# A recommendation tower on one core: tail order, scratch rectangles and batch sizes changed

## The chip, the cores and the metric

The kernel runs on one core of a Trainium2 chip. The metric is the device time of one execution in microseconds; for each kernel several executions are timed and the median is taken. Beside it stands one profiled execution, whose trace gives the start, the length and the waits of each instruction.

## The reference

The inputs are 2048 samples: a dense vector of 128 numbers each, and 26 ids, each naming a row of 128 numbers in its own table (tables of 1000 to 125000 rows). For each sample there are so 27 vectors of 128. What is computed:

```
combined = concat([dense, e_0 .. e_25])            # 27 vectors of 128 per sample
inter    = combined @ combined^T                   # 27 x 27 per sample
z        = concat([dense, inter[upper triangle]])  # 128 + 351
h        = concat([z, dense])                      # 607
h        = relu(h @ W_top1 + b_top1)               # 512
h        = relu(h @ W_top2 + b_top2)               # 256
y        = h @ W_top3                              # 1
```

All of it is in fp32.

## The kernel before, in words

The 2048 samples go through in 8 chunks of 256 (CHUNK), each of two tiles of 128. Of the 27 vectors of a sample, 17 are gathered by GpSimd, one indirect DMA per field and tile (`gather`, line 393), in batches (BATCH_SIZES, line 39); 9 come from small tables kept on chip, looked up by a product of the table with a mask of equal ids (`look_up`, line 429, the masks made by VectorE in `make_masks`); one is the dense vector.

A gathered batch has samples on partitions. TensorE transposes it into one PSUM bank (`turn`, line 415: one transpose for each row of the batch, after `rows_loaded` of the batch and after ScalarE has evicted the batch before), and ScalarE evicts it into `vectors` (`keep_batch`, line 775). So a tile takes five turns and five evictions. GpSimd refills the place of a batch once the batch two tiles back has been turned.

The products of a chunk are made in four steps of 64 samples (`multiply`, line 448: one small product of 27 by 27 for each sample, four samples side by side on the partitions, the "quads"). Step 0 waits for all batches of the chunk's first tile, step 2 for all of the second. Each step is copied into `products` (`keep_step`), by ScalarE but for the very last step, which VectorE copies.

The upper triangle must come to lie with pairs on partitions. For this SP writes `products` to a scratch in DRAM, two rectangles for each quad (`write_quad`, line 215: 26 by 26 and 13 by 13 pairs, each element a run of samples), and loads the 351 pairs back in the order of the first layer's weights (`load_pairs`). For a middle chunk that happens one chunk later than the products: the write starts once the fourth step is kept, and the first layer of chunk i - 1 stands in the middle of chunk i.

The order of each engine's work is written out by hand, as one list for each engine, with waits on semaphores. On TensorE a chunk is: turns of the even tile between look-ups (`chunk`), then `end_of_chunk`: first-layer blocks of the chunk before (`first_layer`, line 465, four of them), step products and turns of the odd tile in alternation, then the second layer, and the last two steps.

The last chunk has a tail of its own (`end`, line 548): its 256 samples go in two halves of 128. The first half is written and loaded as soon as two of four steps are kept (`write_last(0)` and `load_last(0)` on SP); the second half is written by SP (two quads) and ScalarE (two quads) and loaded by SP. `first_of_half` is the first layer of a half in four blocks, `rest_of_half` the second layer and the final product. VectorE keeps the blocks of the first half (`end`, line 690), ScalarE those of the second (`keep_last`, line 838). The output of each half is stored by SP.

Of the kernel before, what the change touches and what calls it, by code (L numbers as in the profile page):

```python
# [16 lines left out]
VECTORS = FIELDS + 1  # L17
DENSE = VECTORS - 1
PAIRS = VECTORS * (VECTORS - 1) // 2
DELTAS = VECTORS // 2  # L20
# [5 lines left out]
LAST = CHUNKS - 1  # L26
# [9 lines left out]
CHUNK_STEPS = TILES * TILE_STEPS  # L36

BATCH_SIZES = (4, 4, 3, 3, 3)
TILE_ROWS = len(GATHERED)  # L40
TILE_BATCHES = len(BATCH_SIZES)
assert sum(BATCH_SIZES) == TILE_ROWS
# [28 lines left out]
MTILES1, MTILES2 = HIDDEN1 // 128, HIDDEN2 // 128  # L71
# [3 lines left out]
HALF = CHUNK // HALVES  # L75
# [4 lines left out]
WRAP = VECTORS + DELTAS - 1  # L80
SLOT = QUADS * CHUNK_GROUPS
SLOTS = VECTORS * WRAP + (VECTORS + 1) * (VECTORS - 1) + 1
FIRST_SLOT = VECTORS * (WRAP - DELTAS)
QUAD_DMAS = 2
SCRATCH_DMAS = QUAD_DMAS * QUADS

# [18 lines left out]
def build(nc, dense, ids, ids_of_field, tables, w1, b1, w2, b2, w3, out):  # L106
    fp32, fp32r, int32 = mybir.dt.float32, mybir.dt.float32r, mybir.dt.int32
    ALU, ACT = mybir.AluOpType, mybir.ActivationFunctionType
# [4 lines left out]
    with ExitStack() as ctx:  # L113
# [101 lines left out]
        def write_quad(engine, c, q, written, half=None):  # L215

            groups = slice(0, CHUNK_GROUPS) if half is None else groups_of(half)

            at = q * CHUNK_GROUPS if half is None else half * HALF + q * HALF_GROUPS
            for rows_, columns, slot in (  # L220
                ((0, VECTORS - 1), (0, VECTORS - 1), VECTORS * (WRAP - VECTORS + 1)),
                ((DELTAS + 1, VECTORS), (VECTORS - DELTAS, VECTORS), (VECTORS + 1) * (DELTAS + 1)),
            ):
                height, width = rows_[1] - rows_[0], columns[1] - columns[0]
                into = bass.AP(scratch[c % 2].tensor, slot * SLOT + at,
                               [[(VECTORS + 1) * SLOT, height], [VECTORS * SLOT, width],
                                [1, groups.stop - groups.start]])
                engine.dma_start(into, products[STRIP * q + rows_[0]:STRIP * q + rows_[1], columns[0]:columns[1], groups])\  # L228
                    .then_inc(written, 16)
# [4 lines left out]
        def samples_of(half):  # L234
            return slice(half * HALF, (half + 1) * HALF)
# [178 lines left out]
        def _(pe):  # L414
            def turn(t, b):

                if t >= ALL_TILES:
                    return
                n = t * TILE_BATCHES + b
                batch = tile_batch(b)  # L420
                pe.wait_ge(rows_loaded[t % TILES * TILE_BATCHES + b], (t // TILES + 1) * 16 * len(batch))
                if n:
                    pe.wait_ge(batch_kept, n)
                for m, v in enumerate(batch):
                    last = nc.tensor.transpose(moved[:, m * TILE:(m + 1) * TILE],  # L425
                                               rows[:, (t * TILE_ROWS + v) % RING, :], identity[:, :])
                last.then_inc(batch_ready, 1)
# [79 lines left out]
            def first_of_half(half, m):  # L507

                firsts, seconds = MTILES1 * (LAST + half), MTILES2 * (LAST + half)
                if m == 0:  # L510
                    pe.wait_ge(half_loaded[half], 16)
                    if half == 0:
                        pe.wait_ge(dense_kept, CHUNKS)
                        pe.wait_ge(second_kept, seconds)
                        pe.wait_ge(y_kept, LAST)
                if m >= 2:
                    pe.wait_ge(first_kept, firsts + m - 1)
                for k in range(KTILES):
                    height = PAIR_ROWS if k < PAIR_TILES else DIM
                    last = nc.tensor.matmul(mlp[:, m % 2, 0:HALF], w1_sb[0:height, k, m * 128:(m + 1) * 128],  # L520
                                            features[0:height, k, samples_of(half)],
                                            start=(k == 0), stop=(k == KTILES - 1))
                last.then_inc(first_ready, 1)

            def rest_of_half(half):

                firsts, seconds = MTILES1 * (LAST + half), MTILES2 * (LAST + half)
                pe.wait_ge(step_kept, CHUNKS * CHUNK_STEPS)
                if half:
                    pe.wait_ge(second_kept, seconds)  # L530
                for k in range(MTILES1):
                    pe.wait_ge(first_kept, firsts + k + 1)
                    for m in range(MTILES2):
                        last = nc.tensor.matmul(banks[:, m, 0:HALF], w2_sb[:, k, m * 128:(m + 1) * 128],
                                                hidden1[:, k, samples_of(half)],
                                                start=(k == 0), stop=(k == MTILES1 - 1))
                        if k == MTILES1 - 1:
                            last.then_inc(second_ready, 1)
                if half:
                    pe.wait_ge(y_kept, LAST + half)  # L540
                for m in range(MTILES2):
                    pe.wait_ge(second_kept, seconds + m + 1)
                    last = nc.tensor.matmul(banks[0:1, MTILES2, 0:HALF], w3_sb[:, m:m + 1],
                                            hidden2[:, m, samples_of(half)],
                                            start=(m == 0), stop=(m == MTILES2 - 1))
                last.then_inc(y_ready, 1)

            def end():

                second_layer(LAST - 1, 1)  # L550
                last_layer(LAST - 1)
                turn(ALL_TILES - 1, TILE_BATCHES - 1)
                first_of_half(0, 0)
                multiply(LAST, 2)
                first_of_half(0, 1)
                first_of_half(0, 2)
                multiply(LAST, 3)
                first_of_half(0, 3)
                rest_of_half(0)
                for m in range(MTILES1):  # L560
                    first_of_half(1, m)
                rest_of_half(1)
# [77 lines left out]
        def _(dve):  # L640
# [41 lines left out]
            def first_of_half(m):  # L682

                if m == 0:
                    dve.wait_ge(second_ready, MTILES2 * LAST)
                dve.wait_ge(first_ready, MTILES1 * LAST + m + 1)
                nc.vector.tensor_scalar(hidden1[:, m, samples_of(0)], mlp[:, m % 2, 0:HALF], b1_sb[:, m:m + 1], 0.0,
                                        ALU.add, ALU.max).then_inc(first_kept, 1)

            def end():  # L690
                for m in range(3):
                    first_of_half(m)
                keep_step(LAST, CHUNK_STEPS - 1)
                first_of_half(3)
                dve.wait_ge(out_written, 16 * HALVES * LAST)
                for m in range(MTILES2):
                    dve.wait_ge(second_ready, MTILES2 * LAST + m + 1)
                    nc.vector.tensor_scalar(hidden2[:, m, samples_of(0)], banks[:, m, 0:HALF], b2_sb[:, m:m + 1], 0.0,
                                            ALU.add, ALU.max).then_inc(second_kept, 1)
                dve.wait_ge(y_ready, LAST + 1)  # L700
                nc.vector.tensor_copy(
                    hidden2[0:1, 1, samples_of(0)].rearrange("o (g q) -> o q g", q=QUADS),
                    banks[0:1, MTILES2, 0:HALF].rearrange("o (q g) -> o q g", q=QUADS)).then_inc(y_kept, 1)

            def keep_dense(c):
                if c:
# [44 lines left out]
        def _(act):  # L751
# [86 lines left out]
            def keep_last():  # L838

                firsts, seconds = MTILES1 * (LAST + 1), MTILES2 * (LAST + 1)  # L840
                samples = samples_of(1)
                for m in range(MTILES1):
                    act.wait_ge(first_ready, firsts + m + 1)
                    nc.scalar.activation(hidden1[:, m, samples], mlp[:, m % 2, 0:HALF], ACT.Relu,
                                         bias=b1_sb[:, m:m + 1]).then_inc(first_kept, 1)
                for m in range(MTILES2):
                    act.wait_ge(second_ready, seconds + m + 1)
                    nc.scalar.activation(hidden2[:, m, samples], banks[:, m, 0:HALF], ACT.Relu,
                                         bias=b2_sb[:, m:m + 1]).then_inc(second_kept, 1)
                act.wait_ge(y_ready, LAST + 2)  # L850
                nc.scalar.activation(
                    hidden2[0:1, 1, samples].rearrange("o (g q) -> o q g", q=QUADS),
                    banks[0:1, MTILES2, 0:HALF].rearrange("o (q g) -> o q g", q=QUADS), ACT.Copy).then_inc(y_kept, 1)
# [149 lines left out]
```

## Time and profile before

| | |
|---|---|
| median of 3 runs | 381.74 us (379.86 to 381.86) |
| profiled execution, device time | 380.22 us |
| its span | 378.1 us |
| mean granted clock of TensorE | 0.973 |
| TensorE busy | 88% of the span |
| VectorE, ScalarE, GpSimd busy | 54%, 50%, 68% |
| HBM read, written | 37.91 MB, 6.93 MB |

The span runs from the first to the last instruction. Busy shares are means over stages with different limits; the chain of waits follows the work that ended last back to the start, and shows which engine held the span at each time. A small idle time between GpSimd's gathers is part of their issue.

### The profile page before, as it was taken

The page shows a single profiled execution, that of the slowest core. Times are in us where ns is not written, and L with a number is a line of the kernel's source. Part 1 is how long each engine was busy: PE and PEld are TensorE (multiplying, and loading weights), DVE is VectorE, ACT ScalarE, POOL GpSimd, SP SyncE. Part 2 cuts the span into 40 slices and gives each one's busy share as a digit, 9 for nine tenths or more (in the row PEclk, how much of TensorE's full clock was granted, in tenths as well). Part 3 has the DMA queues.
Part 4 walks back from the last instruction along what each step waited for, and adds up shares of the span by engine and source line. Part 5 has one row for each costly group of instructions (what it writes and reads, how often), then busy time and mean ns, then how long its engine had stood idle before and what let it go on. Part 6 is the DMA issues. An engine that isn't in the chain of part 4 may idle for free.

```text
span 378.1 us, 13454 instructions
## 1 busy us (share of the span) xinstructions
PE 333.2 (88%) x6048; PEld 298.7 (79%) x6048; DVE 205.1 (54%) x372; ACT 189.2 (50%) x226; POOL 257.9 (68%) x280
## 2 busy tenths in 40 slices
PE   0478767999999899999999899999999999999937
PEld 0467647997899688987899679987899779987737
DVE  3799815891188505980288507970488308900210
ACT  3698543366455464546464464455355554555202
POOL 6777777777777777777777777777777777771000
PEclk9998978899999999999999999999999999999987
DMA  6999528672247422672246422672257223623040
GB/s 180 246 250 203 168 53 234 153 234 53 57 94 185 155 51 60 143 234 55 55 103 179 154 50 64 139 234 56 53 128 237 69 54 86 156 53 68 23 65 2
DMA packets 55414, 45.72 MB, mean 121 GB/s; under 512 B 39443, under 2 KB 45178, under 8 KB 55358
## 3 DMA queue, kind: packets, MB, share of 16 engines
q1 hardware_dynamic: 44912, 26.80, 27.8%
q0 software_dynamic: 8704, 17.84, 17.9%
q8 instruction: 48, 0.79, 0.8%
q10 hardware_dynamic: 1742, 0.22, 0.4%
q14 instruction: 8, 0.07, 0.1%
HBM read 37.91 MB, written 6.93 MB: 119 GB/s over the span
## 4 chain that ended last, share of the span: by engine, by line
PE 83%; DMA 4%; issue 4%; ACT 4%; DVE 3%; SPq 1%; ACTq 1%; DVEq 0%
PE banks L442 39%; PE banks L461 14%; PE mlp L480 12%; PE moved L425 8%; PE mlp L490 6%; PE mlp L520 3%; DMA scratch<-products 2%; DVE masks L660 2%; DMA features<-scratch 1%; DVE low L647 1%; DMA hot_ids<-in_ids_of_field_dram 1%; ACT vectors L787 1%; PE mlp L501 1%; SPq L228 1%; ACT hidden L815 1%
## 5 line engine op out<-in xcount | busy, mean ns | idle before, releaser
L400 POOL DMA_INDIRECT rows<-in_tbl_dram,ids_sb x272 | 257.0, 945 | 83.8 <-issue 81.4
L660 DVE TENSOR_TENSOR masks<-hot_ids,row_of 125x512 fp32r<-125x512 int32 (+1 forms) x336 | 184.8, 617 | 96.7 <-PE banks L442 84.1
L442 PE MATMUL banks<-masks,high 125*128 125x256 f32 x592 | 151.8, 295 | 17.2 <-DVE low L647 17.1
L442 PE MATMUL banks<-masks,low 125*128 125x256 f32 x592 | 147.9, 288 | 0.0
L442 PEld LDWEIGHTS banks<-masks,high 125*128 125x128 f32 x592 | 116.9, 197 | 18.2 <-issue 15.0
L442 PEld LDWEIGHTS banks<-masks,low 125*128 125x128 f32 x592 | 116.9, 197 | 0.0
L787 ACT ACTIVATE vectors<-moved 128x384 f32<-128x384 f32 (+1 forms) x80 | 86.9, 1086 | 5.0 <-PE moved L425 4.7
L770 ACT ACTIVATE vectors<-banks 128x512 f32<-128x512 f32 (+1 forms) x40 | 44.5, 1111 | 78.2 <-PE banks L442 78.2
L461 PEld LDWEIGHTS banks<-vectors 128*27 128x27 f32 x4096 | 45.0, 105 | 22.5 <-issue 17.5
L461 PE MATMUL banks<-vectors 128*27 128x27 f32 x4096 | 54.7, 194 | 8.3 <-issue 3.7
L480 PE MATMUL mlp<-features,w_sb 117*128 117x256 f32 x224 | 53.5, 379 | 0.4 <-issue 0.4
L425 PE MATMUL moved<-identity,rows 128*128 128x128 f32 x272 | 45.4, 282 | 8.5 <-ACT vectors L787 5.5
L800 ACT ACTIVATE products<-banks 123x432 f32<-123x432 f32 x31 | 28.9, 932 | 46.0 <-PE banks L461 46.0
L480 PEld LDWEIGHTS mlp<-features,w_sb 117*128 117x128 f32 x224 | 40.2, 190 | 5.4 <-issue 1.0
L425 PEld LDWEIGHTS moved<-identity,rows 128*128 128x128 f32 x272 | 30.9, 141 | 15.8 <-issue 13.6
L490 PE MATMUL mlp<-hidden,w_sb 128*128 128x256 f32 x112 | 27.0, 386 | 1.7 <-ACT hidden L815 1.7
L490 PEld LDWEIGHTS mlp<-hidden,w_sb 128*128 128x128 f32 x112 | 20.2, 190 | 5.5 <-ACT hidden L815 3.3
L815 ACT ACTIVATE hidden<-mlp,b_sb 128x256 f32<-128x256 f32 x28 | 13.3, 474 | 12.7 <-PE mlp L480 12.4
L669 DVE COPY vectors<-dense_sb 128x256 f32<-128x256 f32 x8 | 3.8, 470 | 28.7 <-PE banks L461 28.7
L520 PE MATMUL mlp<-features,w_sb 117*128 117x128 f32 (+1 forms) x64 | 11.0, 344 | 5.9 <-DMA features<-scratch 5.9
L520 PEld LDWEIGHTS mlp<-features,w_sb 117*128 117x128 f32 (+1 forms) x64 | 10.3, 253 | 6.5 <-DMA features<-scratch 6.4
L827 ACT ACTIVATE hidden<-mlp,b_sb 128x256 f32<-128x256 f32 x14 | 6.6, 474 | 14.7 <-PE mlp L490 14.7
(37 smaller groups left out, 61.4 us busy)
## 6 DMA issues: line engine op xcount, KB each, us to landing
hot_ids<-in_ids_of_field_dram SPq DMA_DIRECT2D x32, 256.0 KB, 4.8
scratch<-products SPq DMA_DIRECT2D x28, 169.0 KB
rows<-in_tbl_dram,ids_sb POOLq DMA_INDIRECT x272
features<-scratch SPq DMA_DIRECT2D x7, 351.0 KB
w_sb<-in_tbl_dram SPq DMA_DIRECT2D x3, 448.0 KB
scratch<-products SPq DMA_DIRECT2D x28, 42.2 KB
hot_ids<-in_ids_of_field_dram SPq DMA_DIRECT2D x8, 128.0 KB
dense_sb<-in_dense_dram SPq DMA_DIRECT2D x8, 128.0 KB, 5.5
```

Of the source, the lines that this page charges most:

```text
L400: pool.indirect_dma_start(rows[:, (tile * TILE_ROWS + v) % RING, :], None, tables[f][:, :], bass.IndirectOffsetOnAxis(ap=ids_sb[:, tile, f ...
L425: last = nc.tensor.transpose(moved[:, m * TILE:(m + 1) * TILE], rows[:, (t * TILE_ROWS + v) % RING, :], identity[:, :])
L442: last = nc.tensor.matmul(banks[:, j % BANKS, m * CHUNK:(m + 1) * CHUNK], part[:, part_of(j * PAIR + m, k), :], masks[:, mask % MASK_RING, ...
L461: last = nc.tensor.matmul(banks[to:to + VECTORS, s, g * VECTORS:(g + 1) * VECTORS], one, one, start=True, stop=True, tile_position=(0, to))
L480: last = nc.tensor.matmul(mlp[:, m % 2, 0:CHUNK], w1_sb[0:height, k, m * 128:(m + 1) * 128], features[0:height, k, :], start=(k == 0), sto ...
L490: last = nc.tensor.matmul(mlp[:, m, 0:CHUNK], w2_sb[:, k, m * 128:(m + 1) * 128], hidden1[:, k, :], start=(k == 0), stop=(k == MTILES1 - 1))
L520: last = nc.tensor.matmul(mlp[:, m % 2, 0:HALF], w1_sb[0:height, k, m * 128:(m + 1) * 128], features[0:height, k, samples_of(half)], start ...
L660: nc.vector.tensor_tensor(masks[:, mask % MASK_RING, 0:size], hot_ids[0:PART_ROWS, n % ID_RING, 0:size], row_of[0:PART_ROWS, row:row + 1]. ...
L770: nc.scalar.activation(of_chunk(c, TILE_ROWS + j * PAIR, WIDTHS[j]), banks[:, j % BANKS, 0:WIDTHS[j] * CHUNK] .rearrange("d (v t s) -> d v ...
L787: nc.scalar.activation(vectors[:, at:at + TILE, batch[0]:batch[-1] + 1].rearrange("d s v -> d v s"), moved[:, 0:len(batch) * TILE].rearran ...
L800: nc.scalar.activation(products[0:PRODUCT_ROWS, ::-1, first:first + STEP_GROUPS].rearrange("p x g -> p g x"), banks[0:PRODUCT_ROWS, s, 0:S ...
L815: nc.scalar.activation(hidden1[:, m, :], mlp[:, m % 2, 0:CHUNK], ACT.Relu, bias=b1_sb[:, m:m + 1])\
```

## The change

The batches of gathered rows are 4, 4, 4, 4 and 1 instead of 4, 4, 3, 3 and 3. The scratch write has three rectangles for each quad instead of two: 13 by 25, 13 by 13 and 13 by 13; the semaphore counts follow from QUAD_DMAS. In the tail TensorE's order of step products and first-layer blocks changes, and VectorE's order of keeps with it. Of the second half's two blocks of the second layer ScalarE keeps the first and VectorE the second, and the final product waits for both.

```
-BATCH_SIZES = (4, 4, 3, 3, 3)
+BATCH_SIZES = (4, 4, 4, 4, 1)
...
-QUAD_DMAS = 2
+QUAD_DMAS = 3
...
             for rows_, columns, slot in (
-                ((0, VECTORS - 1), (0, VECTORS - 1), VECTORS * (WRAP - VECTORS + 1)),
+                ((0, DELTAS), (1, VECTORS - 1), VECTORS * (WRAP - VECTORS + 2)),
+                ((DELTAS, VECTORS - 1), (0, DELTAS), VECTORS * (WRAP - VECTORS + 1) + (VECTORS + 1) * DELTAS),
                 ((DELTAS + 1, VECTORS), (VECTORS - DELTAS, VECTORS), (VECTORS + 1) * (DELTAS + 1)),
...
                 for m in range(MTILES2):
-                    pe.wait_ge(second_kept, seconds + m + 1)
+                    pe.wait_ge(second_kept, seconds + (MTILES2 if half else m + 1))
...
                 turn(ALL_TILES - 1, TILE_BATCHES - 1)
+                multiply(LAST, 2)
                 first_of_half(0, 0)
-                multiply(LAST, 2)
                 first_of_half(0, 1)
+                multiply(LAST, 3)
                 first_of_half(0, 2)
-                multiply(LAST, 3)
                 first_of_half(0, 3)
...
             def end():                                  # VectorE
-                for m in range(3):
-                    first_of_half(m)
+                first_of_half(0)
+                first_of_half(1)
                 keep_step(LAST, CHUNK_STEPS - 1)
+                first_of_half(2)
                 first_of_half(3)
...
+                m = MTILES2 - 1
+                dve.wait_ge(second_ready, MTILES2 * (LAST + 1) + m + 1)
+                nc.vector.tensor_scalar(hidden2[:, m, samples_of(1)], banks[:, m, 0:HALF], b2_sb[:, m:m + 1], 0.0,
+                                        ALU.add, ALU.max).then_inc(second_kept, 1)
...
             def keep_last():                            # ScalarE
-                for m in range(MTILES2):
+                for m in range(MTILES2 - 1):
```

## Rows read from the trace of the kernel before

**Rows 1.** Page: busy us, share, instructions; granted clock in 40 slices, tenths.
```profile
PE 333.2 (88%) x6048; PEld 298.7 (79%) x6048; DVE 205.1 (54%) x372; ACT 189.2 (50%) x226; POOL 257.9 (68%) x280
...
PEclk9998978899999999999999999999999999999987
```
**Rows 2.** Page: the chain that ended last, shares of the span by engine.
```profile
PE 83%; DMA 4%; issue 4%; ACT 4%; DVE 3%; SPq 1%; ACTq 1%; DVEq 0%
```
**Rows 3.** Chain in order of time, first chunk: start us, us, what.
```profile
34.35 0.77 ACT vectors L787
...
51.65 0.76 ACT vectors L787
...
52.55 0.89 PE moved L425 x3
...
56.51 5.01 PE banks L442 x32
```
**Rows 4.** Chain, odd tile of chunk 6 and the next first layer.
```profile
304.17 0.48 ACT hidden L815
...
306.69 0.33 PE moved L425 x3
...
332.95 1.73 PE mlp L480 x8
```
**Rows 5.** Chain, tail.
```profile
341.89 0.32 SPq L228
...
345.17 3.78 DMA scratch<-products
...
348.96 2.42 DMA features<-scratch
...
352.59 1.20 PE banks L461 x83
353.79 1.98 PE mlp L520 x16
...
356.63 0.69 PE banks L461 x44
...
358.29 0.65 ACTq L228
...
360.71 3.50 DMA scratch<-products
...
366.75 6.68 PE mlp L520 x32
...
375.54 0.61 PE banks L543 x4
```
**Rows 6.** Windows: stretch, its us, busy us per engine, PEclk, DMA share, GB/s.
```profile
51.90:58.70 6.80, 5.13 (x141) 4.61 (x142) 0.84 (x2) 2.36 (x3) 5.28 (x6) 0.50 0.25 61
358.30:365.90 7.60, 2.70 (x21) 2.03 (x20) 1.33 (x4) 0.00 (x0) 0.00 (x0) 1.00 0.51 69
365.90:372.70 6.80, 5.95 (x28) 5.96 (x29) 0.00 (x0) 1.10 (x3) 0.00 (x0) 0.50 0.05 15
```
**Rows 7.** Lines by form, ScalarE's evictions: count, busy us, mean ns, idle before.
```profile
L787 ACT ACTIVATE vectors<-moved 128x384 f32<-128x384 f32 x48 | 46.9, 978 | 2.1 <-PE moved L425 1.8
L787 ACT ACTIVATE vectors<-moved 128x512 f32<-128x512 f32 x32 | 40.0, 1249 | 2.9 <-PE moved L425 2.9
```
**Rows 8.** Line 400, the gathers: ns min/median/max, first and last start us.
```profile
L400 POOL DMA_INDIRECT rows<-in_tbl_dram,ids_sb x272: 940/944/1099, 2.8 to 341.5; - x136
```
**Rows 9.** Timeline, SP in the middle and ScalarE in the tail: start us, us.
```profile
317.72 7.20 SPq L228 DMA_DIRECT2D scratch<-products  x8
327.40 0.30 SPq L285 DMA_DIRECT2D features<-scratch  x1
...
351.01 0.93 ACT L787 ACTIVATE vectors<-moved 128x384 f32<-128x384 f32 x1
```
**Rows 10.** Line 228, SP's issues of scratch writes: ns min/median/max, first, last start.
```profile
L228 SPq DMA_DIRECT2D scratch<-products x68: 317/532/2277, 64.6 to 360.7; - x68
```

## The prediction

> **What bounds the kernel now.** I began with the page's busy shares and slices [rows 1]: TensorE works 88% of the span, at the full clock nearly everywhere. The chain of waits [rows 2] agrees: 83% of it is TensorE. So a change pays only where TensorE stands still on the chain. Its pieces in order of time show three such places: the first chunk [rows 3], where evictions by ScalarE stand between TensorE's pieces; the second half of each later chunk [rows 4]; and the tail after the last look-up [rows 5]. In the tail the chain leaves TensorE twice for a scratch write and the load behind it. At the second, TensorE has nothing to do for over 5 us before 366.75, and the 32 first-layer products after that take 6.68 us, against 1.98 for 16 earlier. The windows show why: a granted clock of 0.50, that is 1.2 instead of 2.4 GHz, from 365.9 to 372.7, after a stretch with TensorE busy for 2.70 of 7.60 us [rows 6].
>
> **1. Batches of 4, 4, 4, 4, 1.** A tile keeps 17 transposes and 5 evictions. By form, an eviction of four rows takes 1.25 us and one of three 0.98 [rows 7], so a row is 0.27 and an eviction of one row, on that line, 0.44. A transpose is 0.11 (three in 0.33 [rows 4]).
>
> First chunk [rows 3], where five such evictions are on the chain or beside it: the third of the first tile (34.35) grows by 0.27 and the turn behind it by 0.11; the fifth shrinks by 0.54. On the second tile the third turn grows by 0.11, the fourth eviction (51.65) by 0.27, the turn at 52.55 falls from three transposes to one (0.22 less at least, 0.6 at most, as the row is 0.89; I take 0.3), and the last eviction shrinks by 0.54. The third step product then starts 0.62 sooner (0.38 - 0.54 + 0.11 + 0.27 - 0.3 - 0.54). I book 0.5, as other stalls there may eat a little. Bounds: 0.4 lost (the growth of 0.38 alone counts), 1.1 won.
>
> Later chunks [rows 4]: in the odd tile the third turn gains a transpose on the chain, +0.11. The fourth gains one too, but it lies beside ScalarE's keep of the last first-layer block (0.48), which TensorE waits for anyway; four transposes are 0.44, so the cover just holds. The fifth turn (306.69) loses 0.22. Net 0.1 saved a chunk, 0.6 in six. If the cover fails, another 0.11 takes that gain away. The third eviction, now four rows, must end before the fourth turn: a first-layer block (1.73) lies over its 1.25. In the even tile the turns sit behind look-ups, and their sum does not change: nothing. Bounds: 1.2 won, 0.7 lost (a transpose more in each of six).
>
> Gathers: the fourth batch now needs row 16 of 17, two gathers later, 2.5 us at 1.25 each ((341.5 - 2.8) / 271 [rows 8]). The last tile's row 16 is the last gather but one, over by 341.3. Its turn comes more than a first-layer block after the first-half write starts at 341.89, so after 343.6; some 2 us are left for the landing. Cost nothing, up to 1 us if the kernel gets much faster.
>
> **2. Three rectangles.** 26x26 + 13x13 = 845 elements a quad become 13x25 + 13x13 + 13x13 = 663, 22% fewer, but a chunk issues 12 DMAs instead of 8 on SP. In the middle, 8 issues take 7.20 us from 317.72, and the load of the pairs is issued at 327.40 [rows 9]. TensorE asks for it at 332.95 [rows 4]. A half load lands in 2.42 [rows 5], so the whole takes 2.4 to 4.8, and 0.7 to 3.1 us are spare. Were the write limited by the elements moved, it would shrink by 22% of 9.7, 2.1 us. Were it limited by issue, four more at 0.90 (7.20/8) would add 3.6. Single issues run from 0.32 to 2.28, median 0.53 [rows 10]: the long ones look like a queue that is full, and fewer elements fill it less. I take no cost in the middle. Behind the load SP queues hot ids and the store; VectorE makes masks a good part of a chunk ahead, so nothing waits for them.
>
> **3. Tail, first write** [rows 5]. The first issue begins at 341.89, the last at 345.17, 0.47 apart. Twelve put the last at 347.06; with the same 3.78 and 2.42 behind it the half is there at 353.3, with 22% off the 3.78 at 352.4.
>
> **4. Tail, order.** Before: the eviction of the last batch starts at 351.01 [rows 9], but then the first-layer block waits for the load and is over at 352.59; the product step (1.20), two blocks (1.98) and the last step, from 355.77 to 357.32, follow [rows 5]. After: the eviction of one row, 0.93 less 0.54, starting 0.1 later, ends at 351.5. The product step ends at 352.75, two blocks 1.98 later, and the last step, 1.55, at 356.28: 1.04 sooner. The load (352.4 to 353.3) is needed at 352.75: 0.1 booked, 0.55 at most. The two blocks that move behind the last step run beside the second write, which has some 6 us. VectorE's keep of the last step now stands behind two bias steps instead of three, over by then. SP's store behind the first load gates VectorE only at the second layer, well after.
>
> **5. Tail, second write** [rows 5]. SP and ScalarE issue six each instead of four. From the first issue at 358.29 to the landing at 364.21 are 5.92 us. With two more issues at 0.47, 0.94 more; with 22% fewer elements and nothing else, 1.3 less. The DMA engines are 51% busy there [rows 6], so neither decides alone; I take 0.3 less. ScalarE's issues end well before its next keep, which follows 366.75.
>
> **6. Clock.** TensorE's idle before the second half shrinks by some 1.3 us (1.04 + 0.3). At the full clock 32 products would take 3.96 (twice 1.98), so the low clock cost 2.7. Where its stretch begins and ends I cannot place: 0.3 won, between 0.5 lost and 1.7 won.
>
> **7. Two engines keep the end.** ScalarE's two last keeps go side by side, so the four final products (0.61 at 375.54 [rows 5]) need no second wait between them: 0.1 saved, between 0.2 saved and 0.15 lost by waiting for both.
>
> **Sum.** 0.5 + 0.6 + 1.04 - 0.1 + 0.3 + 0.3 + 0.1 = 2.74, say 2.8. The profiled execution took 380.22 us (span 378.1 and 2.1 around it), so 377.4 there. It lies 1.5 under the median of the runs, 381.74; the forecast for the median is **378.9**.
>
> **Rivals.**
> - *The number of issues decides in the tail.* For: issues stand 0.47 apart in the first write, large and small alike. Against: transfers go on long after the last issue. The second write costs 0.94 instead of winning 0.3, the first load is 0.55 late, the clock wins nothing: 2.8 less 2.0, 0.8 won, 380.9.
> - *Batches win nothing*: the cover in the odd tile fails, and what the first chunk wins is waited for elsewhere. 2.8 less 1.1: 380.0.
> - *Slower: the middle write is bound by issue.* Place: the load of pairs in front of the first layer, in six chunks. Price: 3.6 later against about 1.9 spare, 1.7 in each, 10 us, less the 2.8: 389. It decides once that load is issued after some 329.3 by this chunk's time. For: 0.90 an issue there. Against: fewer elements should empty the queue.
> - *Slower: every DMA pays a time of its own, one after the other.* Place: the tail's writes. The first took 7.06 us for 8, 0.88 each, so four more put its load at 354.9, 2.1 late; the second 5.92 for 4 a queue, two more cost 3.0. 2.74 - 3.3 - 2.0 - 0.3 = 2.9 lost: 384.6. Against: a transfer begun at 345.17 still lands 3.78 later, so they overlap.
> - *Gains in the clock.* With less idle in the first chunk the low stretch from 51.9 to 58.7 [rows 6] goes too: the look-up there took 5.01 [rows 3] instead of the 3.8 usual later, 1.2 won, and 1.4 more of the tail's 2.7: 376.3. Against: idle remains at both places.
>
> The Trainium skill ("DMA: Bandwidth & Descriptors", section "Anatomy of one DMA") gives each DMA a fixed cost of some 2 us, most of it the receipt of the last write, which speaks for the fourth rival: by that figure two more a queue would cost the second write 4 us, and the sum would be a loss of about 4. The trace disagrees with it as a serial cost.
>
> **Chances.** Forecast 0.52 (its own range 377.5 to 380.2), issues in the tail 0.17, no gain from batches 0.12, slower middle 0.05, serial DMAs 0.04, clock 0.10. What this measurement can tell from no change is about 0.5%, 1.9 us: faster means below 379.8. The forecast gives 0.48 of that and the clock 0.10; its rest, the first two rivals make 0.33 within 0.5%; the slower ones 0.09. Faster 0.58, same 0.33, slower 0.09. The range 376.3 to 381.8 leaves out the two slower cases and the ends of the others.
>
> **What would show it.** The last step product ending 1 us sooner against the start of the first-half write; turns of one transpose and evictions near 0.44; twelve issues a chunk, with the pairs' load no later than 9.7 us after the first; the second write within 5 to 6 us; the low clock covering less of the last blocks. The forecast is wrong if the write phases grow, if TensorE waits for the pairs' load in the middle, or if the odd tile's fourth turn waits for an eviction.

## The result, and the profile after

The changed kernel took 376.4 us (median of 4 runs, 375.77 to 377.0) against 380.8 (4 runs, 379.6 to 381.86): ratio 0.9885, 95% interval [0.9842, 0.9929], so 2.7 to 6.0 us less. Forecast: 378.9, range 376.3 to 381.8. The profiled execution's span fell from 378.1 to 374.0.

The same kernel was compared twice more, on two different chips: 1.0019 [0.9975, 1.0063] and 0.9898 [0.9862, 0.9934]. The ratios are taken over the undisturbed executions (in the second comparison without 9 of 35 of the kernel before and one of 12 of the changed one) and so differ a little from the quotient of the medians. By means over all executions but one of some 600 us of either kernel, both in the second comparison, the three give 4.4, 0.9 (379.0 and 378.1) and 3.4 us: about 3, near the forecast's 2.8. But the first two intervals do not meet, so the size of the gain is known only as some 1 to 4 us. The first result was at the lucky end, 0.1 above the lower bound of the range; 0.9 of the 2.5 us by which it lies under the forecast is the kernel before, which took 380.8 there and not 381.74.

The page after, in the lines of [rows 1 and 2]:

```profile
PE 331.2 (89%) x6048; PEld 297.7 (80%) x6048; DVE 205.6 (55%) x373; ACT 188.8 (50%) x225; POOL 257.9 (69%) x280
...
PEclk9999988899999999998999999999999999999988
...
PE 83%; DVE 5%; ACT 4%; issue 4%; DMA 3%; ACTq 1%; SPq 0%; DVEq 0%
```

It looks like before: still TensorE's kernel. The difference is in the chain's pieces (start us, us, what). First chunk, against [rows 3]:

```profile
33.65 1.02 ACT vectors L793
...
51.08 1.01 ACT vectors L793
...
52.22 0.31 PE moved L426
...
52.56 0.43 ACT vectors L793
...
54.80 5.07 PE banks L443 x32
```

The evictions on the chain have grown from 0.77 and 0.76 to 1.02 and 1.01, the turn of three transposes (0.89) is one of 0.31, and the last eviction is 0.43. From the third eviction's start to the third step product (54.44 before, 53.04 after) 20.09 us have become 19.39. The remaining 0.7 us by which this chunk is ahead was there at the third eviction, before anything changed: the kernel before had a low-clock stretch (granted clock 0.5) from 28.0 to 31.4 in that execution. That stretch lies ahead of the first batch whose size changed, so the change cannot have moved it: five of the six profiles with the old batches have it, and three of the eight with the new.

A later odd tile, against [rows 4]:

```profile
300.53 0.63 PE moved L426 x4
...
302.92 0.48 ACT hidden L821
...
305.44 0.11 PE moved L426
...
331.21 1.73 PE mlp L481 x8
```

The third turn has four transposes, the fifth one; the keep of 0.48 between them still covers the fourth. From the third turn to the end of the second layer each odd tile takes 6.73 to 6.76 us instead of 6.84 to 6.92: some 0.11 less in each of chunks 1 to 6. In the last chunk the fifth turn stands behind the second layer, and there the same stretch is 0.11 longer (6.64 instead of 6.53).

The tail, against [rows 5]:

```profile
348.78 0.29 ACT vectors L793
...
349.12 1.27 PE banks L462 x83
...
350.41 2.02 PE mlp L521 x16
352.43 1.41 PE banks L462 x99
...
357.69 2.69 DMA scratch<-products
...
360.45 2.55 DMA features<-scratch
...
363.04 6.08 PE mlp L521 x32
369.12 1.80 PE banks L535 x16
...
370.94 0.36 DVE hidden L708
...
371.44 0.61 PE banks L544 x4
```

The load of the first half is gone from the chain: step product, two blocks, step product run without a wait. After the second write the 32 products still take 6.08, and the windows (columns as in [rows 6]) still show half the clock over most of them:

```profile
358.50:360.90 2.40, 0.01 (x1) 0.00 (x0) 0.37 (x1) 0.00 (x0) 0.00 (x0) 1.00 0.35 45
360.90:367.80 6.90, 4.76 (x22) 4.76 (x23) 0.00 (x0) 0.73 (x2) 0.00 (x0) 0.51 0.09 26
```

### The profile page after: what moved, and what is told of

Read it like the earlier page. It is cut to its first block, busy times and chain, and to the rows that moved or that the text cites. A ratio compares the mean times of both kernels' runs of the same rounds, so it can differ in the third digit from the quotient of the medians.

```text
span 374.0 us, 13490 instructions
## 1 busy us (share of the span) xinstructions
PE 331.2 (89%) x6048; PEld 297.7 (80%) x6048; DVE 205.6 (55%) x373; ACT 188.8 (50%) x225; POOL 257.9 (69%) x280
## 3 DMA queue, kind: packets, MB, share of 16 engines
q0 software_dynamic: 8704, 17.84, 17.9%
## 4 chain that ended last, share of the span: by engine, by line
PE 83%; DVE 5%; ACT 4%; issue 4%; DMA 3%; ACTq 1%; SPq 0%; DVEq 0%
PE banks L443 37%; PE banks L462 14%; PE mlp L481 13%; PE moved L426 8%; PE mlp L491 7%; DVE masks L661 3%; PE mlp L521 2%; DVE low L648 2%; DMA hot_ids<-in_ids_of_field_dram 1%; ACT vectors L793 1%; PE mlp L502 1%; ACT hidden L821 1%; ACTq L229 1%; DMA scratch<-products 1%; DMA features<-scratch 1%
## 5 line engine op out<-in xcount | busy, mean ns | idle before, releaser
L793 ACT ACTIVATE vectors<-moved 128x512 f32<-128x512 f32 (+1 forms) x80 | 86.8, 1084 | 5.9 <-PE moved L426 5.9
L462 PE MATMUL banks<-vectors 128*27 128x27 f32 x4096 | 53.9, 194 | 7.2 <-issue 3.2
L481 PE MATMUL mlp<-features,w_sb 117*128 117x256 f32 x224 | 54.6, 387 | 0.0
L481 PEld LDWEIGHTS mlp<-features,w_sb 117*128 117x128 f32 x224 | 41.2, 194 | 4.7
L521 PE MATMUL mlp<-features,w_sb 117*128 117x128 f32 (+1 forms) x64 | 10.2, 329 | 4.6 <-DMA features<-scratch 4.5
```

What stands on the lines that cost most here:

```text
L462: last = nc.tensor.matmul(banks[to:to + VECTORS, s, g * VECTORS:(g + 1) * VECTORS], one, one, start=True, stop=True, tile_position=(0, to))
L481: last = nc.tensor.matmul(mlp[:, m % 2, 0:CHUNK], w1_sb[0:height, k, m * 128:(m + 1) * 128], features[0:height, k, :], start=(k == 0), sto ...
L793: nc.scalar.activation(vectors[:, at:at + TILE, batch[0]:batch[-1] + 1].rearrange("d s v -> d v s"), moved[:, 0:len(batch) * TILE].rearran ...
```

## The experiments

Four kernels with one part each, timed together.

**Batches alone.** `BATCH_SIZES = (4, 4, 4, 4, 1)`.

> Only the batches are 4, 4, 4, 4, 1; all else as before. My theory: of the 4.1 us by which the changed kernel's span is shorter, about 0.8 come from the first chunk's evictions (third step product against the third eviction) and 0.11 from each of the seven odd tiles, so 1.5 us less in all, 379.3 if before is 380.8; in the trace each odd tile's third turn adds 0.11 and the fifth takes off 0.22. Rival (the batches win nothing, the first chunk was luck of that execution): the time stays within 0.5 us of before, and the third step product starts no sooner against the third eviction of the first tile.

Measured: 379.41 against 380.18, ratio 1.0001 [0.9965, 1.0038]. Up to the last chunk the trace does what was expected: from the third turn of the odd tile to the second layer's end 6.73 to 6.76 us in chunks 1 to 6, and the third step product 17.9 us after the first tile's fourth turn instead of 19.2. In the last odd tile TensorE waits 0.47 us for a gathered row, the last of the fourth batch (chain, the transfer and the turn behind it):

```profile
340.44 3.12 DMA rows<-in_tbl_dram,ids_sb
...
343.60 0.66 PE moved L425 x4
```

The stretch takes 6.93 us there, and the last step ends 15.60 us after the start of the first write, against 15.41 before: nothing won in the tail. The time shows none of the gain clearly; what it should be, 0.996, lies just outside the interval. I come back to this.

**Rectangles alone.**

```
-QUAD_DMAS = 2
+QUAD_DMAS = 3
...
-                ((0, VECTORS - 1), (0, VECTORS - 1), VECTORS * (WRAP - VECTORS + 1)),
+                ((0, DELTAS), (1, VECTORS - 1), VECTORS * (WRAP - VECTORS + 2)),
+                ((DELTAS, VECTORS - 1), (0, DELTAS), VECTORS * (WRAP - VECTORS + 1) + (VECTORS + 1) * DELTAS),
```

> Only the three rectangles (12 writes a chunk of 663 elements a quad instead of 8 of 845). My theory: issue and elements balance; the second half's write takes 5.6 us instead of 5.9, the first half's 7.2 instead of 7.1, the middle load comes no later; 0.3 us less, not to be told from no change. Rival A (number of issues decides): the second write takes 6.9, the first 8.6 or more, 1 to 1.5 us slower. Rival B (elements decide): 4.7 and 5.5 us, 1.3 us faster.

Measured: 378.03, ratio 0.9966 [0.9929, 1.0002]. From the first issue to the load's issue: second write 5.63 us (5.99 before), first write 7.59 (7.08), the middle ones 9.5 on average (9.85). So neither rival. But the chain shows a price that the old order pays:

```profile
348.89 2.59 DMA features<-scratch
...
351.53 1.16 PE mlp L521 x8
```

The first write ends later, and TensorE waits 1.13 us for its load in front of the first block (0.45 in the kernel before). The new order is what makes twelve issues harmless there: in none of the eight profiles that have both does TensorE wait for that load.

**Order alone** (the tail's lists on TensorE and VectorE, as in the diff).

> Only the order of step products and first-layer blocks in the tail (TensorE) and of the keeps (VectorE). My theory: the last eviction still has three rows and ends at 351.9 by the clock of before, so the last step product ends 0.6 us sooner, and the time is 0.6 us less. Rival (the load of the first half gates the block anyway): the last step product ends as late as before against the start of the first half's write, no gain.

Measured: 379.86, ratio 0.9997 [0.9957, 1.0038]. From the last turn to the start of the last step product: 4.82 us, against 5.27 before, 4.90 with the batches alone, and 4.09 with both, in all seven profiles that have both. The chain shows why:

```profile
352.12 0.93 ACT vectors L788
...
353.10 1.27 PE banks L461 x83
```

With three rows the eviction (0.93 here, 0.29 on the changed kernel's chain) holds the product back once the load does not; the whole eviction of one row takes 0.42. The last step itself took 2.0 us in this execution (1.6 before), 0.53 of it a wait of the kind explained under the last experiment, which ate the gain in this execution.

**Shared keep alone** (VectorE keeps the second block; the final product waits for both).

> Only the second half's second-layer keeps shared between ScalarE and VectorE, the final product waiting for both. From the changed kernel's trace: no gain, 0.53 us from the end of the second layer to the final product as before, and 0.61 for the product: 0.0 us. Rival (my prediction): 0.1 less.

Measured: 381.08, ratio 1.0006 [0.9969, 1.0043]. From the first product of the second half's second layer to the final product 2.48 us, against 2.28 in the three above: 0.2 lost, not 0.1 won.

**The changed kernel again.**

> The changed kernel once more, timed in more executions. Each part alone moved the time by 0.3% at most, and none was told from no change. My theory (the parts add up, and the batch of one and the order win more together, as the last eviction is then short): 3 to 4 us less than before, ratio about 0.991. Rival (the first comparison was lucky): the parts' sum of 0.4%, ratio about 0.996.

Measured: 378.62 against 378.95, ratio 1.0019; see above. In its trace the parts are as in the first (6.73 to 6.76, 4.09, second write 5.61); the first chunk had one low-clock stretch more, 36.8 to 40.2, under a look-up that took 5.33 us instead of 3.85, and a later one was twice as long (53.9 to 60.7).

**The changed kernel without the batches.**

> The changed kernel with the old batches (4, 4, 3, 3, 3). My theory: 2 to 2.5 us slower than the changed kernel: 0.8 in the first chunk, 0.11 in each of seven odd tiles, and 0.6 to 0.8 in the tail, where the last eviction of three rows holds the product step back; from the last turn to the end of the last step product 6.2 us instead of 5.5. Rival (the batches won nothing): less than 0.5 us slower.

Measured: 378.06, ratio 0.9993 [0.9959, 1.0028], beside 378.62 for the changed kernel in the same comparison: no slower. The trace shows what was expected of it (odd tiles 6.84 to 6.87 in chunks 1 to 6; last turn to the last step's end 6.1 us), but by the time the rival holds here.

**Products in the idle stretch.** The last low clock was tested by keeping TensorE busy.

```
                 rest_of_half(0)
+                for n in range(32):
+                    nc.tensor.matmul(banks[:, 3, 0:HALF], w2_sb[:, n % MTILES1, 0:128],
+                                     hidden1[:, n % MTILES1, samples_of(0)], start=True, stop=True)
                 for m in range(MTILES1):
                     first_of_half(1, m)
```

Measured: 377.37, ratio 0.9972 [0.9937, 1.0007]. Chain:

```profile
360.70 7.34 PE banks L562 x64
368.05 3.57 PE mlp L521 x32
```

From the load's issue to the second layer it is 8.9 us, against 8.7 in the changed kernel timed beside it: the theory held for the clock, and the second rival ate its gain.

This execution was early in the middle, and there it paid for the new batches. In the odd tiles of chunks 5 and 6 TensorE waited 0.89 and 3.21 us for the last gathered row of the fourth batch, and behind the longer wait the clock fell (0.5 from 303.7 to 307.1), so that a second-layer block took 3.10 us instead of 1.7 to 2.0:

```profile
298.57 4.19 DMA rows<-in_tbl_dram,ids_sb
...
302.80 0.66 PE moved L426 x4
303.46 3.10 PE mlp L491 x8
```

Together the two tiles were 5.6 us longer than 6.75 each.

**The same, with ScalarE keeping both blocks.**

> As the kernel with the 32 added products, but ScalarE alone keeps the second half's second layer, as before the change. From the trace of the keep alone: from the first product of the second half's second layer to the end of the final product 2.9 us instead of 3.1, so 0.2 us less than with two engines; if all that is right this is the fastest, 5 us or more under the kernel before. Rival (my prediction): 0.1 us more.

Measured: 377.08, ratio 0.9956 [0.9921, 0.999]. The keep's 0.2 is back (2.28), the delay stays.

**The changed kernel a third time.**

> The changed kernel a third time, since the first two comparisons disagree (ratios 0.9885 and 1.0019, intervals that do not meet). Theory one (a real gain of 2 to 3 us, moved up and down by how many low-clock stretches each execution draws, about 1.25 us each): ratio 0.992 to 0.996. Theory two (nothing but those draws): 0.999 or more. Theory three (the first result is the size): 0.989 or less.

Measured: 377.08 against 380.67, ratio 0.9898 [0.9862, 0.9934], between theories one and three.

**Fourteen products, one engine keeps.** As above with `range(14)` and the keep of the kernel before.

> The changed kernel with 14 added products on TensorE (28 matmuls in the trace, 3.3 us at 0.117 each) in place of 32 (64 matmuls, 7.2 us, which ended 2.8 us after the load), and with ScalarE alone keeping the second half's second layer. My theory: they end some 0.9 us before the load lands, the clock stays up, the second half's first layer takes 3.6 us instead of 5.3 to 6.7, and the load gates it again: 2.3 us less than the changed kernel, 0.2 of it from the keep... Rival (the last 1 us of idle lets the clock fall all the same): 5 us or more for the first layer, no gain but the keep's.

Measured: 374.06, ratio 0.9832 [0.9792, 0.9872], the fastest: 6.6 us under the kernel before and 3.0 (2.4 by means) under the changed one in the same comparison. Timeline (start us, us, in brackets the idle time before) and windows:

```profile
360.90 3.39 PE L562 MATMUL banks<-hidden,w_sb 128*128 128x128 f32 x28
365.31 3.84 PE L521 MATMUL mlp<-features,w_sb 117*128 117x128 f32 x32 [1.02 <-DMA features<-scratch]
```

```profile
361.30:365.30 4.00, 3.00 (x27) 2.80 (x26) 0.09 (x1) 0.00 (x0) 0.00 (x0) 1.00 0.31 65
365.30:369.00 3.70, 3.69 (x33) 3.69 (x34) 0.00 (x0) 1.10 (x3) 0.00 (x0) 1.00 0.02 4
```

**The changed kernel, ScalarE keeps both blocks.**

> The changed kernel with ScalarE alone keeping the second half's second layer. My theory: 2.28 us from the first product of the second half's second layer to the final product's start instead of 2.48; the time cannot tell 0.2 us from no change. Rival: 2.48 as with two engines, the loss comes from elsewhere.

Measured: 377.54, ratio 0.991 [0.9878, 0.9943]. Its chain, and that of the changed kernel beside it:

```profile
370.94 1.58 PE banks L535 x14
...
372.54 0.38 ACT hidden L850
...
373.05 0.61 PE banks L544 x4
```

```profile
371.37 1.80 PE banks L535 x16
...
373.19 0.36 DVE hidden L708
...
373.69 0.61 PE banks L544 x4
```

2.11 us from the second layer's piece to the final product with one engine, 2.32 with two. With one, the first final product starts once the first block is kept, and the second block's keep runs beside it. With two, VectorE's keep begins only when the second block is made (370.94 in the changed kernel, 0.2 after ScalarE's), and nothing starts before it ends.

**Twelve writes of all the elements.** The 26 by 26 rectangle of the kernel before as two of 13 by 26.

```
-QUAD_DMAS = 2
+QUAD_DMAS = 3
...
-                ((0, VECTORS - 1), (0, VECTORS - 1), VECTORS * (WRAP - VECTORS + 1)),
+                ((0, DELTAS), (0, VECTORS - 1), VECTORS * (WRAP - VECTORS + 1)),
+                ((DELTAS, VECTORS - 1), (0, VECTORS - 1), VECTORS * (WRAP - VECTORS + 1) + (VECTORS + 1) * DELTAS),
```

> The kernel before with its 26 by 26 rectangle written as two of 13 by 26: 12 writes a chunk, but all 845 elements a quad. With 8 writes the second half's write and the first half's took 6.0 to 6.2 and 6.8 to 7.2 us to the load's issue, with 12 of 663 elements 5.6 and 7.1 to 7.7. Theory one (elements move the second write, the number of issues only the first): 6.0 to 6.3 for the second, 7.2 to 7.8 for the first. Theory two (each adds its own): 6.5 to 7 and 8 or more. Theory three (smaller rectangles are cheaper for another reason than elements): 5.6 for the second.

Measured: 386.95, ratio 1.0188 [1.0139, 1.0236]. Second write 6.48 us, first 7.41, middle ones 10.7 to 12.6. SP's timeline in one chunk, then the chain there:

```profile
238.62 9.50 SPq L229 DMA_DIRECT2D scratch<-products  x12
251.08 0.30 SPq L286 DMA_DIRECT2D features<-scratch  x1
```

```profile
251.08 3.91 DMA features<-scratch
...
255.03 2.00 PE mlp L481 x8
```

Here the middle load does gate TensorE, by 0.9 us in this one of seven chunks, as the slower rival had it. With the kernels on either side it separates the two prices (ranges over the profiles of each kind):

| to the load's issue, us | 8 writes, 845 (4 profiles) | 12 writes, 845 (1) | 12 writes, 663 (9) |
|---|---|---|---|
| middle, mean of seven | 9.8 to 10.0 | 11.6 | 9.2 to 9.6 |
| first half | 6.8 to 7.2 | 7.41 | 7.1 to 7.7 |
| second half | 6.0 to 6.2 | 6.48 | 5.6 to 5.7 |

In the middle four more writes cost 1.6 to 1.8 us, and 22% fewer elements give back 2.0 to 2.4; in the second half it is 0.3 to 0.5 and 0.8 to 0.9. In the first half the kinds overlap, and the two prices cannot be told apart.

The Trainium skill ("DMA: Bandwidth & Descriptors", section "Anatomy of one DMA") gives a fixed cost of some 2 us for one DMA of the kind that GpSimd issues, and puts most of it into the wait until the last byte is known to have landed. For the writes here, which SP and ScalarE issue, such a cost does not add up from one DMA to the next: two more on each queue cost the second write 0.3 to 0.5 us. The prediction let that figure speak for its fourth rival as if it were serial; the section does not say that.

The profiled execution is 4.6 us longer than that of the kernel before. The middle load adds 0.9, the wait for the first half's load 0.4, and waits of TensorE for which the profile shows no cause ("issue"), up to 2.5 us each, 4.4; the last first layer, with less low clock, gives 0.9 back. That DMA traffic delays TensorE's own instructions was my guess. The traces show half of it: the kernel's instructions come in by DMA too, in packets of 16 KB, as the page of the kernel before lists them (packets, MB, share of 16 engines' span):

```profile
q8 instruction: 48, 0.79, 0.8%
```

From 45 us on the 14 profiles have 94 such waits over 0.15 us, and each ends 1.2 to 1.6 us after one of these packets has been moved. They stand at 13 places of TensorE's program, five of them in all 14 profiles, and the places lie multiples of 256 instructions apart (to within one, counted with weight loads and waits). So TensorE waits there for its next instructions: 4.5 to 7.7 us in each of the other profiles, 10.6 in this one. That the longer writes delayed these packets fits, but one profile does not show it.

## Why the prediction was right, point by point

- *Batches, first chunk* (0.5 booked, 0.62 worked out): 0.70 between the two traces. The turn of one transpose was mis-sized: 0.58 less, 0.3 taken; 0.2 of that went to step products that took longer in this execution. Over all profiles, from the start of the third eviction to the third step product, the six with the old batches take 20.3 to 22.0 us (mean 20.9) and the eight with the new 19.3 to 22.7 (mean 20.4), so 0.5.
- *Batches, odd tiles* (0.6): some 0.11 in each, 0.7 in six; the last one lost 0.1. The cover held.
- *Gathers* (nothing, up to 1 us if the kernel gets much faster): right in the first trace after, but not in all. Two of the eight profiles with the new batches wait for a gathered row, for 0.47 us and for 4.1 in all. The step took some 2 us from the end of the gather's issue as enough for the landing; the gathers that were waited for landed 2.5 to 4.2 us after the start of theirs, so hardly anything was spare.
- *Middle write* (nothing): the load is issued 9.2 us after the first write instead of 9.85 (means of seven chunks). Right, but as a balance of two large terms, not because issue is cheap.
- *First write* (0.1): no wait in the new order. 7.25 instead of 7.08.
- *Order* (1.04): the last step ends 14.20 us after the start of the first write instead of 15.41, 1.21 sooner. From the last turn to the start of the last step product it is 1.18, 0.45 of it from the order alone.
- *Second write* (0.3): 0.33 less, the load 0.1 longer. The bounds were too wide: issue 0.3 to 0.5, elements 0.8 to 0.9.
- *Clock* (0.3): from the first of the 32 products to the second layer 6.52 us before and 5.91 after in the first two traces, with 5.45 and 4.53 us of idle ahead of them. Over the profiles 5.3 to 6.7, mean 6.05, with the old order (five), and 5.2 to 6.6, mean 6.01, with the new one (six, without the two with 64 matmuls and the one with 28): the shorter idle gained 0.1 at most, within a spread as wide as the range given. What decides is how much of the low-clock stretch lies over the products, 3.2 to 6.4 us in these eleven (mean 5.0 and 4.9), half of which is lost. The 0.6 of the first two traces was luck.
- *Two engines keep the end* (0.1 won): failed. 0.2 lost, in each of the six profiles that have it. The step took the wait for the second keep as exposed; it lay beside the first final product.

The measured parts make 2.7 us (0.7 + 0.7 + 1.2 + 0.2 + 0.1 - 0.2), as forecast in sum, not in each part. The spans of the two first traces differ by 4.1; the excess is stretches of low clock and waits for instructions that fell differently in the two executions (0.7 us before the third eviction, 0.5 in the tail's clock, 0.2 in between).

What stays open is why the timings do not show the batches' share, some 1.2 us by the means of the traces (0.5 and 0.7): alone they gained nothing, and without them the changed kernel was no slower. 1.2 us would be a ratio of 0.997, which the interval of the batches alone does not exclude. Against it stands what the gathers cost. Before, the fourth turn of the last tile began 6.2 to 12.0 us after GpSimd issued the last row for it (six profiles); with the new batches it begins 2.7 to 5.2 us after (eight). GpSimd issues the last row but one at 340.2 to 341.2 us of the span in all 14 profiles, at its own pace of 1.25 us a gather, so an execution in which TensorE comes early has to wait there. How much of the missing time that makes was not measured.

Executions of one kernel spread by 5 us and more, and their time goes with their mean granted clock: over 35 of the kernel before, a fit gives 2.7 us less for each 0.01 more (correlation -0.77). In the first chunk TensorE's idle at the third eviction, 1.9 to 3.2 us with the new batches and 1.8 in five of six profiles with the old, looks like a price of the longer eviction, but most of it is not. Where the stretch of low clock at some 28 to 33 us is there, the idle is 1.8 and 1.9; where it is not, it is 2.3 to 3.2, and 2.9 in the one profile with the old batches. Three of the eight profiles with the new batches and one of the six others have a low-clock stretch between 34 and 41 us, and these four are the slowest of their kind in that chunk. Whether the new batches make it more frequent was not shown.

## What to carry to other kernels

When a write becomes more and smaller pieces, price the number and the elements apart, at each place where the write stands; the same change cost or gave some 2 us in the middle and under 1 us at the end. When a consumer takes larger batches, ask when the last row of each lands, not when it is issued: the slower engine that feeds it may have been close behind. Sharing two short keeps between engines does not pay where the first consumer needs only the first of them. A wait that cannot be shortened may still be filled: a few products that nobody reads kept the clock up for the work behind it, and from the load's issue to the second layer it became 6.1 us instead of 7.8 to 9.1, against 1.2 won by the reordering.

## What the runs showed of the hardware

The same bytes in 12 writes instead of 8 kept SP issuing for 9.50 us against 7.37 in the same chunk of the kernel before, and over seven chunks the write was on average 1.6 to 1.8 us longer. From their first to the second layer, TensorE's 32 first-layer products took 3.57 to 3.67 us when the engine had been busy until at most 1 us before, and 5.2 to 6.7 after 4.4 to 5.9 us of idle. A gather for which TensorE waited landed 2.5 to 4.2 us after the start of its issue. Waits of TensorE for its own instructions, up to 2.5 us each, make 4.5 to 10.6 us of each profile, and end 1.2 to 1.6 us after a packet of 16 KB. Mean clock and time of single executions move together; which of them moves the other was not shown, and the spread has to be averaged out over many executions, and over chips.
